# Two of four token blocks routed and scattered inside the last 20 attention steps, and three other reorderings, in a two-layer adaLN block on one Trainium2 core

## What is computed

```python
h = _layernorm(x) * (1 + ca) + sa
x = x + ga * _L0_attn_ref(h, ...)      # spectral attention and convolution
h = _layernorm(x) * (1 + cb) + sb
x = x + gb * _L0_ffn_ref(h, ...)       # ternary: silu(w1 x)*(w2 x), gelu(h1 .), gelu(h2 .), w3
...
attn = softmax(einsum('bhqd,bhkd->bhqk', q, k) * SCALE)
x = x + ga * (out @ fc_w.T + fc_b + h)
h = _layernorm(x) * (1 + cb) + sb
score = relu(h @ rw1 + rb1) @ rw2 + rb2
_, topi = top_k(score, 2)
gate = softmax(where(mask, score, -inf))
for e in range(8):
    out = out + gate[:, e:e+1] * (relu(h @ W1[e] + b1[e]) @ W2[e] + b2[e])
x = x + gb * out
```

## Time and profile before

| quantity | value |
|---|---|
| median of 3 runs | 1128.51 us (1125.94 to 1132.19) |
| profiled execution, its own time | 1128.35 us |
| span of its trace | 1126.5 us |
| mean granted PE clock | 0.954 |
| busy, share of the span | PE 92%, DVE 74%, ACT 71%, POOL 15% |
| chain that ended last | DVE 49% (L1662 alone 42%), PE 40%, issue 4%, ACT 4%, DMA 2% |

### The profile page before, as it was taken

The page is one execution under the profiler, slowest core; times in us unless marked ns, Lnnn a source line. Parts: engine busy times, 40 slices in busy tenths (PEclk is TensorE's granted clock), DMA queues, the critical chain, the costliest instruction groups (busy, mean ns, idle before and its releaser), DMA issues.

```text
span 1126.5 us, 21109 instructions
## 1 busy us (share of the span) xinstructions
PE 1033.0 (92%) x8426; PEld 559.5 (50%) x8426; DVE 829.9 (74%) x1170; ACT 799.4 (71%) x1542; POOL 172.5 (15%) x217
## 2 busy tenths in 40 slices
PE   3878889989999999999999999999999998869995
PEld 3645668763433333333333333333333447748984
DVE  4768433368879999999999999999999306144544
ACT  2655543447579999999999999999999784107664
POOL 1002000016470000000000000000000102543552
PEclk9899999999989999999999999999999998659997
DMA  7000000000000101100110111011000000135653
GB/s 288 1 1 0 1 1 0 1 1 1 1 1 2 30 3 31 31 24 9 31 31 13 20 31 31 2 30 31 2 1 2 2 2 3 40 100 172 201 171 121
DMA packets 35952, 41.19 MB, mean 37 GB/s; under 512 B 2924, under 2 KB 27119, under 8 KB 35472
## 3 DMA queue, kind: packets, MB, share of 16 engines
q1 hardware_dynamic: 33072, 32.83, 10.6%
q0 software_dynamic: 2496, 4.27, 1.1%
q10 hardware_dynamic: 288, 2.76, 0.6%
HBM read 25.36 MB, written 15.15 MB: 36 GB/s over the span
## 4 chain that ended last, share of the span: by engine, by line
DVE 49%; PE 40%; issue 4%; ACT 4%; DMA 2%; another core or an unknown queue 1%; POOL 0%; POOLq 0%; SPq 0%; DVEq 0%; ACTq 0%
DVE mx L1662 42%; PE ps L982 5%; PE ps L983 4%; PE ps L984 4%; PE ps L1171 4%; PE ps L1109 4%; PE ps L1354 3%; PE ps L1056 3%; PE ps L1078 2%; PE ps L963 2%; PE ps L1019 1%; PE ps L1256 1%; DMA x<-x_in 1%; PE ps L910 1%
## 5 line engine op out<-in xcount | busy, mean ns | idle before, releaser
L1662 DVE TENSOR_REDUCE mx<-ps 128x2 f32<-128x1024 f32 x512 | 586.3, 1214 | 18.9 <-PE ps L1078 18.8
L761 ACT ACTIVATE probs<-ps 128x512 f32<-128x512 f32 x1024 | 540.9, 598 | 54.1 <-PE ps L1171 46.2
L1171 PE MATMUL ps<-Qb,Ks 32*128 32x512 f32 x1024 | 329.9, 496 | 0.5 <-ACT probs L761 0.5
L1109 PE MATMUL ps<-probs,V 128*16 128x256 f32 x4096 | 320.8, 386 | 7.0 <-ACT U L755 7.0
L1078 PE MATMUL ps<-Ks,Qb 32*128 32x512 f32 x1024 | 255.3, 497 | 1.0 <-DVE mx L1662 0.7
L1171 PEld LDWEIGHTS ps<-Qb,Ks 32*128 32x128 f32 x1024 | 149.4, 182 | 215.0 <-issue 123.3
L1109 PEld LDWEIGHTS ps<-probs,V 128*16 128x16 f32 x4096 | 67.2, 94 | 134.4 <-issue 77.5
L1078 PEld LDWEIGHTS ps<-Ks,Qb 32*128 32x128 f32 x1024 | 95.0, 182 | 34.2 <-DVE mx L1662 18.3
L496 POOL TENSOR_SCALAR mhi<-mn 128x16 fp32r<-128x16 f32 x16 | 4.2, 261 | 422.3 <-DVE mn L1670 422.3
L829 ACT ACTIVATE eh<-ps,b 128x256 f32<-128x256 f32 x92 | 36.7, 477 | 28.4 <-PE ps L984 26.7
L568 POOL DMA_INDIRECT yk<-ye,target x46 | 47.3, 1028 | 57.0 <-DVE ye L1894 45.0
(11 more groups left out here) (302 smaller groups left out, 1313.2 us busy)
## 6 DMA issues: line engine op xcount, KB each, us to landing
w<-moe_in SPq DMA_DIRECT2D x23, 512.0 KB
buf<-zeros SPq DMA_DIRECT2D x11, 792.0 KB, 6.3
gz<-buf SPq DMA_DIRECT2D x23, 132.0 KB
FW<-ffn_in SPq DMA_DIRECT2D x1, 2824.5 KB, 12.4
yin<-yk SPq DMA_DIRECT2D x4, 512.0 KB
SW<-spectral_in ACTq DMA_DIRECT2D x1, 1479.5 KB, 9.3
DW<-mods_in ACTq DMA_DIRECT2D x1, 1219.0 KB, 5.7
x<-x_in SPq DMA_DIRECT2D x4, 256.0 KB, 10.7
```

The costliest lines, as they stand in the source:

```text
L761: act.activation(probs[:, 4 * ((s + 2) % 4) + g, :], score(n), ACT.Exp, scale=SCALE1) \
L1109: last = pe.matmul(ps[32 * g:32 * g + VW, 6, queries], V[:, kt, col:col + VW], probs[:, 4 * ((s + 2) % 4) + g, queries], start=(kt == 0 an ...
L1171: pe.matmul(score(n), Ks[rows, hg, kt * P:kt * P + P], Qb[rows, hg, :], start=True, stop=True).then_inc(sem.st_ready, 1)
L1662: dve.tensor_reduce(mx[:, k // 16 % 2, k % 16 // 4, k % 4, 2 * pair:2 * pair + 2], ps[:, at:at + 2, :], AX, ALU.max).then_inc(sem.bank_rea ...
```

## The change

It has five parts.

1. **Front of the ternary feed-forward.** The layer norm's rows are made in two groups (tiles 0 to 3, then 4 to 15), so ACT's square root for blocks 1 to 3 comes once, between the gates of block 0 and `ffn_b(0)`. PE transposes block 1 inside `ffn_hidden(0, 0)` and blocks 2 and 3 right behind it, then comes `ffn_up(1)`. The second parts of the gate products of blocks 0 and 1 (eight operations of 128x512) go from DVE to POOL; the cast of h2 goes from POOL to ACT, its second part stays on POOL in four pieces.
2. **Stacks.** Block 3's stack of K comes behind the stack of Q rather than ahead of it, with one unread product and block 3's transposes between.
3. **Start of the attention.** PE no longer waits for the cleared bank 6 before step 0. In steps 0 and 1, which have no values, `first_steps` puts two unread matmuls of full height in each of the four places. DVE clears bank 6 at step 2, and PE waits for it there.
4. **Tail and router.** The 40 slots of steps 236 to 255 are now filled by the table `tail`: 27 of them hold work, 13 are empty; `keep_warm` is gone. Behind the output projections of blocks 0 to 2 come `turn_z` of blocks 0 to 2, `router` of blocks 0 and 1 by quarters (three matmuls a slot), their `router_scores` by quarters (four products a slot) and `places` 0 and 1. ACT stays with the exponentials, so DVE does what ACT and POOL did for these blocks: the square root (`root_inverse`, 12 small operations, three Newton steps), `modulated` of blocks 0 to 2, `row_seconds`, relu of blocks 0 and 1. After the attention PE runs the quarters of `router(2)` between `turn_outputs(16)`, `heads(3)` and `fc(3)`, then block 2's scores, block 3's router and scores, with block 2's places between. POOL's split of rw1 comes earlier (behind the 13th group of maxima).
5. **Behind the table** `unread(1, 8)` becomes `unread(1, 3)`, and the unread matmuls in `places` of blocks 2 and 3 are gone.

The diff, cut to what the steps below speak of:

```diff
+        tail = (("heads", 0), ("fc", 0), ("heads", 1), None, ("fc", 1), ("heads", 2), None, ("fc", 2), ("turn_z", 0), None,
+                None, ("router", 0, 0), ("router", 0, 1), ("router", 0, 2), ("router", 0, 3), ("turn_z", 1),
+                ("scores", 0, 0), ("scores", 0, 1), ("scores", 0, 2), ("scores", 0, 3), ("router", 1, 0), ("router", 1, 1),
+                ("places", 0), ("router", 1, 2), ("router", 1, 3), ("scores", 1, 0), ("scores", 1, 1), ("scores", 1, 2),
+                ("scores", 1, 3), ("turn_z", 2), None, ("places", 1)) + (None,) * 8
...
-        stacks = [(0, 0, tb) for tb in range(TB)] + [(1, 0, 0)] + [(0, 1, tb) for tb in range(TB)] \
+        stacks = [(0, 0, tb) for tb in range(TB - 1)] + [(1, 0, 0), (0, 0, TB - 1)] + [(0, 1, tb) for tb in range(TB)] \
...
-        norms = [(k, a, b) for k, parts in enumerate((((0, 16),), ((0, 4), (4, 8), (8, 12), (12, 16)), ((0, 12), (12, 16)), ((0, 12), (12, 16)))) for a, b in parts]
+        norms = [(k, a, b) for k, parts in enumerate((((0, 16),), ((0, 4), (4, 16)), ((0, 12), (12, 16)), ((0, 4), (4, 8), (8, 12), (12, 16)))) for a, b in parts]
+        by_table = [n for n in norms if n[0] < 3 or n[1] == 12]
...
+            for n in range(FB):
+                second_part(n)
...
+            for fb in range(FB):
+                part_h = slice(fb * FF, fb * FF + FF)
+                pool.tensor_tensor(h2_[1][:, part_h], fw["h2"][:, part_h], h2_[0][:, part_h].bitcast(F32), ALU.subtract) \
+                    .then_inc(sem.weight_split, 1)
+            for n in range(FB, 2 * FB):
+                second_part(n)
...
-            for b in range(TB):
-                pool.wait_ge(sem.hT_ready, TB * 2 + b + 1)
-                pool.wait_ge(sem.hT_first, TB + b + 1)
-                block = slice(512 * b, 512 * b + 512)
-                pool.tensor_tensor(hT1[1][:, block], hT[:, block], hT1[0][:, block].bitcast(F32), ALU.subtract) \
-                    .then_inc(sem.hT_second, 1)
...
             ffn_gates(0)
-            act.wait_ge(sem.bcast_ready, 5)
-            act.activation(gb[:, 0:4, :], ps[:, 7, :].rearrange("p (n d) -> p n d", n=4), ACT.Copy).then_inc(sem.bcast_copied, 1)
-            act.activation(gb[:, 4, :], ps[:, 6, 0:P], ACT.Copy).then_inc(sem.bcast_copied, 1)
-            ffn_b(0)
-            ln_std(1, 8)
-            ln_std(1, 12)
-            ffn_gates(1)
-            ffn_c(0)
-            ln_out(1, 2)
-            ln_out(1, 3)
+            ln_std(1, 4)
+            ffn_b(0, (gains, lambda: ln_out(1, 1), split_h2))
+            ffn_gates(1, lambda: ln_out(1, 2))
+            ffn_c(0, lambda: ln_out(1, 3))
...
-            ln_std(3)
-            modulated(0)
-            modulated(1)
-            relu(0, 0)
-            relu(0, 1)
+            act.wait_ge(sem.sc_ready, 1)
+            act.wait_ge(sem.rh_copied, 8)
+            for fb in range(3):
+                relu(2, fb)
             ln_std(3, 12)
-            relu(0, 2)
-            relu(0, 3)
-            modulated(2)
-            modulated(3)
-            for tb in range(1, TB):
-                for fb in range(FB):
-                    relu(tb, fb)
+            relu(2, 3)
+            act.wait_ge(sem.zT_ready, TB * 3)
+            block = slice(512 * 3, 512 * 4)
+            act.activation(hT1[0][:, block], bank(first_turn), ACT.Identity, bias=modv[:, 9:10], scale=cv[:, 3:4]) \
+               .then_inc(sem.hT_first, 1)
+            act.activation(hT[:, block], bank(first_turn), ACT.Identity, bias=modv[:, 9:10], scale=cv[:, 3:4]) \
+               .then_inc(sem.hT_ready, 1)
+            act.wait_ge(sem.sc_ready, 2)
+            for fb in range(FB):
+                relu(3, fb)
...
-            for b in range(2):
-                z_transposes(1, b)
+            z_transposes(1, 0)
...
-            pe.wait_ge(sem.hT_ready, 2)
-            ffn_hidden(0, 0)
-            pe.wait_ge(sem.hT_second, 2)
-            ffn_up(1)
-            pe.wait_ge(sem.weight_split, 2)
-            ffn_hidden(0, 1)
+            ffn_hidden(0, 0, lambda: z_transposes(1, 1))
             pe.wait_ge(sem.bcast_copied, 2)
             z_transposes(1, 2)
             z_transposes(1, 3)
+            pe.wait_ge(sem.hT_second, 2)
+            ffn_up(1)
+            pe.wait_ge(sem.weight_split, 5)
+            ffn_hidden(0, 1)
...
+            def first_steps():
+
+                for _ in range(2):
+                    last = pe.matmul(bank(6), Ks[:, 0, 0:P], Ks[:, 0, 0:512], start=True, stop=True)
+                return last
...
-            def keep_warm():
-
-                for g in (2, 3):
-                    rows = slice(32 * g, 32 * g + 32)
-                    pe.matmul(bank(g), Ks[rows, 0, 0:P], Ks[rows, 0, 0:512], start=True, stop=True)
...
-            keep_busy(2).then_inc(sem.busy_done, 1)
-            pe.wait_ge(sem.busy_done, 1)
-            pe.wait_ge(sem.u_zero, 1)
+            keep_busy(2)
...
+            pe.wait_ge(sem.prod_made, 2)
+            router(2, 0)
             turn_outputs(16)
...
+            router(2, 1)
+            pe.wait_ge(sem.hT_ready, TB * 2 + 3)
             heads(3)
-            turn_z(0)
+            router(2, 2)
             fc(3)
-            turn_z(1)
-            router(0)
-            turn_z(2)
-            router_scores(0)
+            router(2, 3)
+            for qt in range(4):
+                router_scores(2, qt)
             turn_z(3)
-            router(1)
-            places(0)
-            router_scores(1)
-            router(2)
-            places(1)
-            router_scores(2)
-            router(3)
             places(2)
-            router_scores(3)
+            for fb in range(FB):
+                router(3, fb)
+            for qt in range(4):
+                router_scores(3, qt)
             places(3)
...
-            unread(1, 8)
+            unread(1, 3)
...
-            dve.wait_ge(sem.kq_full, len(stacks) - early)
-            dve.wait_ge(sem.v_copied, NT // 2)
-            dve.memset(bank(6), 0.0).then_inc(sem.u_zero, 1)
             for s in range(236):
+                if s == 2:
+                    dve.wait_ge(sem.busy_done, 1)
+                    dve.memset(bank(6), 0.0).then_inc(sem.u_zero, 1)
...
+            def root_inverse(b):
+                mine, at = cols(b, 4), 11 * b
+                y = rstd[:, mine]
+                dve.wait_ge(sem.stats, 32 * 3 + 8 * (b + 1))
+                dve.tensor_scalar(root[:, 0, :], mv[:, mine, 1], 1e-5, None, ALU.add).then_inc(sem.root_step, 1)
+                dve.tensor_scalar(root[:, 1, :], mv[:, mine, 1], 1e-5, -0.5, ALU.add, ALU.mult).then_inc(sem.root_step, 1)
+                dve.wait_ge(sem.root_step, at + 2)
+                dve.tensor_scalar(y.bitcast(I32), root[:, 0, :].bitcast(I32), -0.5, 1597463007.0, ALU.mult, ALU.add) \
+                   .then_inc(sem.root_step, 1)
+                for n in range(3):
+                    dve.wait_ge(sem.root_step, at + 3 + 3 * n)
+                    dve.tensor_tensor(root[:, 2, :], y, y, ALU.mult).then_inc(sem.root_step, 1)
+                    dve.wait_ge(sem.root_step, at + 4 + 3 * n)
+                    dve.tensor_tensor(root[:, 2, :], root[:, 2, :], root[:, 1, :], ALU.mult).then_inc(sem.root_step, 1)
+                    dve.wait_ge(sem.root_step, at + 5 + 3 * n)
+                    dve.scalar_tensor_tensor(out=y, in0=root[:, 2, :], scalar=1.5, in1=y, op0=ALU.add, op1=ALU.mult) \
+                       .then_inc(sem.root_step if n < 2 else sem.ln_z, 1)
+                dve.wait_ge(sem.ln_z, rows_made(3, 4 * b) - 1)
...
             turned(0)
+            residual(0)
+            block_stats(0)
             turned(1)
-            residual(0)
+            root_inverse(0)
+            residual(1)
             turned(2)
-            residual(1)
+            normal(3, 0, 4)
+            block_stats(1)
+            residual(2)
+            modulated(0)
+            twin(0)
+            row_seconds(0)
```

320 lines of the change are left out of this document (198 added, 122 removed).

## The result

| | before | with the change |
|---|---|---|
| median | 1127.40 us (1125.94 to 1132.19) | 1147.95 us (1146.54 to 1149.27) |
| ratio | | 1.0175, interval 1.0141 to 1.0209 |
| profiled execution, span | 1128.35, 1126.5 | 1147.67, 1145.5 |
| mean granted clock | 0.954 | 0.933 |

What follows compares the result with a forecast made beforehand. PE was taken to bound the front, tail and router phase, with waits and low clock, DVE's maxima the untouched middle. From 1128.35 us, -10.0 - 1.5 - 1.5 - 9.0 + 1.6 = -20.4 gave 1108.0 us, range 1098 to 1122.

Steps and rivals of the forecast that it cites:

- Front, stacks: Ternary feed-forward: both long PE waits and half clock go, -10.0 us; K and Q stacks: first wait partly filled, -1.5.
- The third rival: Front: its gain is eaten by DVE and POOL blocking each other, 9.2 us, total 1117.5; chance 0.08.
- Start of the attention: The 12 us from 316: unread matmuls in eight empty places keep the clock up, -1.5 us, bounds 0 to -2.4.
- Tail: Last attention steps, 876 to 930 us before: with router items in the slots takes 74.5 us for 54, +20.5.
- my 43: Tail: DVE's expected work, some 43 us against 74, so DVE covers it and isn't late.
- my 74.5: Tail: its expected length in us, slots and items summed to 73.7 plus 0.8 where ACT's exponentials limit.
- my sign of being wrong: Tail: the prediction would be wrong if it took over 80 us, with DVE late.
- Behind the attention: From the attention's end to the fourth block's slots: 36.5 us, slots at 987 instead of 996, -9; bounds -16 to +2.
- the standstill: Router phase before: DVE gets block 2's finished scores 8.9 us late, cause unknown; forecast not met again; recurring once 0.18.
- Behind the table: Fourth slots to first expert matmul: less unread filler, PE idles longer, experts may start at half clock, +1.6, bounds 0 to +2.
- a standstill at each run of scatters: Scatters of blocks 0, 1 and 2: 8.9 us each, slower than before from the third, 1135; chance 0.09.
- the tail's PE keeps the full clock to the end: Behind the attention: PE's clock stays full, 6.5 us less, total 1101.5; chance 0.08.

Runs made afterwards that it cites:

- the run that held the clock: Changed kernel with spread table, places later, five unread full-height matmuls ahead of each tail score quarter and ten in each of places 0 and 1: 1120.68 us.
- the kernel before (shifted): Kernel before with 256 more already-reached semaphore waits at PE's start, shifting its instruction stream: 1115.55 us on one chip, 1127.90 us on another.
- the run without tail: Changed kernel without parts 4 and 5: front, stacks and start of the attention changed, tail, router phase and unread(1, 8) as before: 1106.4 us, ratio 0.9854.

## Why the prediction was wrong, by its steps

**Front, stacks (-11.5; measured -12.5).** Right within its bounds. By the trace the front alone is -12.1 (block transposes of layer 1 at 230.93 instead of 243.01) and the stacks -0.4 instead of -1.5. Both long waits of the earlier trace rows are gone:

```profile
121.80 0.50 PE L1001 MATMUL ps<-hT,w 128*128 128x512 f32 x1 [0.88 <-DVE af L1642]
122.14 0.39 PE L1002 MATMUL ps<-hT,w 128*128 128x512 f32 x1
```

One wait of 0.88 us stands where 3.68 did, and PE keeps the full clock behind it (0.39 a matmul). The front gained 2.1 us more than its -10.0, and one term of the sum accounts for it: I had set 2.9 us against the gain for a new wait ahead of the first `ffn_b`, and PE has no wait in 108 to 120 us. The stacks' two waits make 2.2 us together instead of the 3.4 of the earlier trace rows:

```profile
237.80 0.66 PE L991 MATMUL ps<-CW,z 128*128 128x128 f32 x4 [0.84 <-DVE z L1441]
239.78 1.69 PE L1076 MATMUL ps<-hT,AW 128*128 128x512 f32 x2 [1.32 <-ACT hT L614]
```

The third rival (DVE and POOL block each other) didn't come, though each moved operation took POOL 1.29 us and not 1.15. DVE's gate products ran at their usual length beside POOL's subtractions (117.64 to 123.1 us), and so did the one product with two SBUF inputs:

```profile
118.75 0.72 DVE L1655 TENSOR_TENSOR act_b<-bf,act_b 128x512 fp32r<-128x512 f32 x1 [1.66 <-ACT bf L720]
...
121.00 0.75 DVE L1642 SCALAR_TENSOR_TENSOR af<-ug,ss,ps 128x512 f32<-128x512 f32 x1
```

0.72 us at 118.75, against 2.53 in the earlier trace rows. The Trainium skill (SBUF — State Buffer, section "SBUF: two separate sides") has the port pair locked for a whole instruction; by that rule cutting POOL's 128x2048 subtraction in four leaves at most one piece to wait for. The trace has none of the long waits, but it tests the rule little: this is the only such product that ran well into a subtraction, and it began 0.2 us before that piece ended.

**Start of the attention (-1.5; measured -0.8 up to step 236).** Right in kind: the clock is 1.00 in 316 to 328 us instead of 0.72.

**Tail (+20.5; measured +58.7). This step failed.** I took every item at its full-clock price because the window of the tail had a clock of 1.00, and I asked only whether DVE would be late. It was not: PE never waits for DVE in the tail of the changed kernel, and DVE was busy for 37.1 us there against my 43. The item prices held too: in the run that held the clock the tail took 89.3 us, less 11.7 of fillers 77.6, against my 74.5. So of the 38.2 us that the tail went over, 3.1 are prices and 35.1 the clock, a term that I had put at nothing. The tail passed the 80 us of my sign of being wrong, but not for the reason that I gave with it (DVE late).

The rows for it were there: block 2's scores took 5.91 us and block 0's 3.89, and the router phase had a clock of 0.72. Nearer still, the kernel before has the four transposes of `turn_z` just ahead of block 0's scores and just behind them:

```profile
940.42 0.62 PE L1235 MATMUL ps<-CW,zx 128*128 128x128 f32 x4
...
945.10 1.09 PE L1235 MATMUL ps<-CW,zx 128*128 128x128 f32 x4
```

They take 0.62 us at full clock and 1.09 behind the products of 8 columns: the fall stood in the trace of before, at the same products. I used these rows for the stretch behind the attention and not for the same products moved into it. The cost is not that of the narrow products (8 quarters x 0.97 us = 7.8 us) but of all that runs behind them: 79 us at half speed.

The Trainium skill (TensorE: Matmul & The Clock Gate, section "Part 1: The HAM clock gate") lets the clock follow how busy PE has been. By PE's busy time alone the clock should have come back in the tail; the trace disagrees, with 77.67 of 79 us busy at 0.51. What the runs here have in common is what PE did before it fell: products of 8 columns in all nine traces in which the clock was lost in the tail, in one of them followed by a wait and products of 24 and 32 columns. In the runs with the tail of before, which have none there, it was not lost; in the run with five fillers, which has them, it was held.

**Behind the attention (36.5; measured 40.8, and 36.3 in the held run).** The mechanism and nearly the size were right. The changed kernel started this stretch at full clock (975.36) and lost it in block 2's scores. What I compared it with was wrong, as the prediction itself had noted: 9 us of gain were the standstill, which the trace of the kernel before (shifted) on another chip doesn't show. There is a small one in the changed kernel too:

```profile
1008.74 0.19 DVE L1823 TENSOR_TENSOR sc<-ps,MW 128x32 f32<-128x32 f32 x1 [12.17 <-remote]
...
1016.05 0.17 DVE L1856 CAST slot<-slot_f 128x8 int32<-128x8 f32 x1
```

PE's records of block 3's scores end at 1006.2 and DVE has them at 1008.74, 2.5 us later. The forecast came near by some luck: it was made of a clock between the two levels, and the stretch ran at full clock up to block 2's scores and at half in block 3's router products.

**Behind the table (+1.6; measured -0.7).** The row of `unread(1, 8)` answers to these:

```profile
1026.88 5.40 PE L983 MATMUL ps<-AW,CW 128*128 128x512 f32 x6 [9.78 <-DVE w1l L1950]
...
1036.61 0.56 PE L1001 MATMUL ps<-ghh,w1h 128*128 128x256 f32 x1
```

Less filler did start the experts at half clock (0.56 for a matmul that took 0.36; the same 0.56 in the other two runs with three fillers and a tail of before, and 0.36 in those with eight), but the loop as a whole took 108.9 us against 109.3, so no loss from it can be seen.

**Chances.** I gave "slower" 0.07, by a mechanism (a standstill at each run of scatters) that didn't come; that some chance stood on "slower" is no merit of the working. The rival that came is one I had only in its friendly form, "the tail's PE keeps the full clock to the end". Its unfriendly half, the clock lost inside the attention, had a price in the rows: the part of the 74.5 us from the first narrow slot on, doubled.

**What the tail is worth with its clock.** From last heads to fourth slots: 112.7 + 40.8 = 153.5 us as changed; 89.3 + 36.3 - 11.7 = 113.9 held and without its fillers (worked out, not run); between 108.3 and 113.2 in the five runs with the old tail and the new front; 120.1 in the kernel before with its standstill and 109.5 in the (shifted) kernel before without it. So by these numbers the move of the router under the attention gains at most what the standstill costs. That fits PE being busy for most of both stretches (53.7 of 54 us and 54.9 of 59 in the run without tail), with the same products to do; no run separates this from the rest.

## What to carry to other kernels

Before moving work into a stage that runs at full clock, look in the trace at what the clock did around that work where it is now. If it fell there, price the whole stage at half speed as a rival. Where the bound engine is the same in both places, hiding work behind a stage doesn't shorten the sum; here the three parts that removed waits and half clock (12.5 and 0.8 us) were all of the gain, and the versions without the tail ran at 0.985 to 0.993 of before. Compare a suspicious gap with the same kernel on a second chip before counting its removal as a gain.
